# Cross-attention block on one core: the last tile of context keys in three passes instead of five, and a new hand-written order of the loop and its ends

## The reference, cut to what matters

```python
def _attn(x, ctx, wq, wk, wv, wo, bo, heads):
    q, k, v = x @ wq, ctx @ wk, ctx @ wv        # split into heads
    sim = jnp.einsum('bhid,bhjd->bhij', q, k) * scale
    a = jax.nn.softmax(sim, axis=-1)
    out = jnp.einsum('bhij,bhjd->bhid', a, v)
    return out @ wo + bo                        # heads joined again
h1 = _ln(x, n1_g, n1_b)
x = _attn(h1, h1, q1, k1, v1, o1_w, o1_b, heads) + x
h2 = _ln(x, n2_g, n2_b)
x = _attn(h2, context, q2, k2, v2, o2_w, o2_b, heads) + x
h3 = _ln(x, n3_g, n3_b)
a, g = jnp.split(h3 @ ff_w1 + ff_b1, 2, axis=-1)
return a * jax.nn.gelu(g, approximate=False) @ ff_w2 + ff_b2 + x
```

## Time and profile before

| | us |
|---|---|
| three runs: median, lowest, highest | 1290.41, 1287.4, 1293.53 |
| the profiled execution: its own time | 1285.88 |
| its span, first to last instruction | 1284.1 |
| PE busy in it | 1224.0 |
| first self scores of the lead-in, of the loop, first exponent of the run-out, first matmul of the feed-forward stage (from the span's start) | 147.93, 191.36, 860.03, 924.05 |

### The profile page before, as it was taken

The page is one execution under the profiler, slowest core; times in us unless marked ns, Lnnn a source line. Parts: engine busy times, 40 slices in busy tenths (PEclk is TensorE's granted clock), DMA queues, the critical chain, the costliest instruction groups (busy, mean ns, idle before and its releaser), DMA issues. The chain is left out here.

```text
span 1284.1 us, 34279 instructions
## 1 busy us (share of the span) xinstructions
PE 1224.0 (95%) x12788; PEld 1127.6 (88%) x12788; DVE 814.2 (63%) x1606; ACT 668.2 (52%) x1622; POOL 601.2 (47%) x792
## 2 busy tenths in 40 slices
PE   5899879999999999999999999998899999999999
PEld 3898768989898888888888988886699999999999
DVE  5554457888787788887888888876565243332521
ACT  5565326666666666666666666664552322323130
POOL 5431235465564654655646556451673433423331
PEclk9999879999999999999999999999899999999999
DMA  4576744544545555455454554532121101010000
GB/s 129 194 237 210 240 155 122 166 152 143 170 139 178 163 156 183 151 167 181 129 174 134 153 165 130 178 107 78 41 63 36 31 11 41 0 51 0 26 1 26
DMA packets 105145, 154.49 MB, mean 120 GB/s; under 512 B 20780, under 2 KB 86564, under 8 KB 104996
## 3 DMA queue, kind: packets, MB, share of 16 engines
q1 hardware_dynamic: 104556, 151.94, 38.2%
q10 hardware_dynamic: 440, 0.54, 0.1%
HBM read 62.98 MB, written 28.93 MB: 72 GB/s over the span
## 5 line engine op out<-in xcount | busy, mean ns | idle before, releaser
L1418 ACT ACTIVATE probs<-expin 120x400 f32<-120x400 f32 (+2 forms) x635 | 293.3, 505 | 132.3 <-PE expin L811 130.3
L1095 DVE TENSOR_REDUCE neg_max<-score 100x2 f32<-100x722 f32 x320 | 288.2, 901 | 100.6 <-PE score L785 99.2
L811 PE MATMUL expin<-qs,ks 128*120 128x200 f32 (+2 forms) x1270 | 197.0, 272 | 6.3 <-ACT probs L1418 3.0
L811 PEld LDWEIGHTS expin<-qs,ks 128*120 128x120 f32 (+2 forms) x1270 | 176.4, 180 | 16.8 <-ACT probs L1418 5.8
L785 PE MATMUL score<-ks,qs 128*100 128x362 f32 x640 | 172.6, 351 | 11.8 <-DVE neg_max L1095 7.4
L1609 POOL MEMSET qs<- 128x2400 f32 (+1 forms) x58 | 112.6, 1941 | 146.5 <-PE expin L811 146.5
L2664 DVE SCALAR_TENSOR_TENSOR hidden<-ps_a,b_cols,gelu 128x320 f32<-128x320 f32 x100 | 55.1, 551 | 166.1 <-PE ps_a L2588 166.0
L2826 POOL TENSOR_TENSOR hid_lo<-hidden,hid_hi 128x320 fp32r<-128x320 f32 x100 | 88.1, 881 | 122.0 <-ACT hid_hi L2734 121.8
L2746 ACT ACTIVATE gelu<-ps_g,b_cols 128x320 f32<-128x320 f32 x100 | 52.7, 527 | 137.8 <-PE ps_g L2588 137.8
L785 PEld LDWEIGHTS score<-ks,qs 128*100 128x100 f32 x640 | 83.6, 166 | 38.4 <-issue 21.0
L833 PE MATMUL attn<-probs,vc 120*17 120x100 f32 (+1 forms) x3840 | 107.9, 251 | 0.0
(11 more groups left out here) (222 smaller groups left out, 2893.1 us busy)
## 6 DMA issues: line engine op xcount, KB each, us to landing
ks<-kc_parts SPq DMA_DIRECT2D x96, 362.0 KB, 4.0
qk_dram<-qk_parts SPq DMA_DIRECT2D x32, 500.0 KB, 5.5
qs<-q_parts SPq DMA_DIRECT2D x192, 75.0 KB
ks<-qk_dram SPq DMA_DIRECT2D x96, 125.0 KB
ctx_raw<-in_ctxT SPq DMA_DIRECT2D x64, 180.5 KB
ks<-kc_parts SPq DMA_DIRECT2D x96, 90.5 KB, 2.7
qs<-qk_dram SPq DMA_DIRECT2D x64, 125.0 KB
vs<-v_dram SPq DMA_DIRECT2D x32, 132.8 KB
```

The lines of the kernel that those rows point to most:

```text
L811: mm = pe.matmul(dst, ks[a][u][:, k_slot(c) if a == 2 else c, j0:j0 + n], qs[a][u][:, :, q_slot(c) if a == 2 else c, :], start=True, stop= ...
L1095: ins = nc.vector.tensor_reduce(dst, src, AX_X, ALU.max, negate=True)
L1418: nc.scalar.activation(probs[e % NPT][0:n, :], expin[e % 2][0:n, 0:HG * N], ACT.Exp, scale=SCALE)\
```

## The change: what it does, and its diff

The weights of the context lie in a new layout: four pieces (high and low of the first 128 features, high twice and low twice of the last 64) for key tiles 0 and 1 and for the values, and a piece of its own, `w_c_last`, for key tile 2. The context's second column block holds its high part in partitions 0 to 63 and its low part in 64 to 127 ("mixed"), and `ctx_lo` has the first 128 features alone. Key tiles 0 and 1 and the values still take five passes. Key tile 2 takes three: high and low weights side by side (128 columns held) against the high context, the high weights (64 columns) against the low context, and 128 columns against the mixed block. Its sum then lies in two halves of the PSUM bank, and DVE adds them with one more instruction in `kc_low`. POOL makes the mixed block with one more instruction for each part of a context.

All five engines get another order. In the loop, self-attention's exponents of groups 0 to 3 of f stand at the end of f's period, not at the start of the next one, and so does the turn of s's maxima; `project_vc(s, 2)` and `turn_max(1, f)` stand between the second self scores and the first cross scores. The lead-in and the run-out are reordered too.

```diff
 def work_jobs(x, s, c, f):
-    order = [("MT2", x, 0), ("VC", s, 2), ("O2", y, 0), ("MT1", f, 0), ("KC", c, 0), ("KC", c, 1), ("O1", c, 0),
-             ("KC", c, 2), ("T2", c, 0), ("Q2", c, 0), ("QT", c, 0), ("VC", c, 0), ("VC", c, 1)]
+    order = [("VC", s, 2), ("MT1", f, 0), ("O2", y, 0), ("KC", c, 0), ("O1", c, 0), ("KC", c, 1), ("T2", c, 0),
+             ("KC", c, 2), ("Q2", c, 0), ("QT", c, 0), ("VC", c, 0), ("VC", c, 1), ("MT2", s, 0)]
...
+        w_c = [at("w_c", [P, 8 * P + 4 * D], early.weights), sb("w_c_last", [P, 2 * P], F32R)]
...
             def run_out():                                        # SP
+                place_kc(30, 0)
                 place_kc(30, 2)
                 place_q2(30)
...
             def period(x, s, c, f, e):                            # SP
                 y = x - 1 if x else None
+                v = y - 1 if y else None
+                place_kc(s, 0)
                 place_q2(s)
                 place_max(2, x)
-                if x is not None and 8 <= x < 8 + FF // P:
-                    load_w1(x - 8)
+                if y is not None and 8 <= y < 8 + FF // P:
+                    load_w1(y - 8)
+                place_kc(s, 2)
+                place_max(1, f)
                 load_context(f)
-                place_kc(s, 2)
+                store_x2(v)
                 load_qkv1(e)
-                load_x(e)
-                place_kc(c, 0)
-                store_x2(y)
-                place_max(1, f)
+                load_x(f)
...
             def project_kc(b, t):                                 # PE
-                dst = bank(job)[0:f1 - f0, 0:JP]
-                pe.matmul(dst, w_c[:, 0, f0:f1], ctx_hi[:, 0, :], start=True, stop=False)
-                pe.matmul(dst, w_c[:, 1, f0:f1], ctx_hi[:, 0, :], start=False, stop=False)
-                pe.matmul(dst, w_c[:, 0, f0:f1], ctx_lo[:, 0, :], start=False, stop=False)
-                pe.matmul(dst, w_c[:, 2, f0:f1], ctx_hi[:, 1, :], start=False, stop=False)
-                done(pe.matmul(dst, w_c[:, 2, f0:f1], ctx_lo[:, 1, :], start=False, stop=True), job)
+                m, hi, lo, mixed = f1 - f0, ctx_hi[:, 0, :], ctx_lo[:], ctx_hi[:, 1, :]
+                dst = bank(job)[:, 0:JP]
+                if t == 2:
+                    w = w_c[1]
+                    pe.matmul(dst[0:2 * m], w[:, 0:2 * m], hi, start=True, stop=False)
+                    pe.matmul(dst[0:m], w[:, 0:m], lo, start=False, stop=False)
+                    mm = pe.matmul(dst[0:2 * m], w[:, 2 * m:4 * m], mixed, start=False, stop=True)
+                else:
+                    passes = ((0, hi), (1, hi), (0, lo), (2, mixed), (3, mixed))
...
             def lead_in():                                        # PE: its start
+                project_out(1, 0)
                 self_scores(1, 0)
-                project_out(1, 0)
+                self_scores(1, 1)
                 project_kc(0, 0)
                 project_vc(0, 0)
                 project_kc(0, 1)
-                self_scores(1, 1)
+                turn_normalised(0)
                 turn_max(1, 1)
-                turn_normalised(0)
                 project_q2(0)
                 turn_q2(0)
+                project_vc(0, 1)
                 self_scores(2, 0)
...
             def run_out():                                        # PE: its start
-                scores_for_exp(1, 31, 0, 0)
-                turn_max(2, 29)
-                scores_for_exp(1, 31, 1, 0)
-                scores_for_exp(1, 31, 2, 0)
-                scores_for_exp(1, 31, 3, 0)
                 scores_for_exp(1, 31, 4, 0)
...
                 project_vc(30, 2)
+                project_out(2, 28)
                 cross_scores(30, 0)
-                project_out(2, 28)
...
             def period(x, s, c, f):                               # PE
                 self_scores(f, 0)
-                scores_for_exp(1, c, 0, 0)
-                turn_max(2, x)
-                scores_for_exp(1, c, 1, 0)
-                project_vc(s, 2)
-                scores_for_exp(1, c, 2, 0)
-                scores_for_exp(1, c, 3, 0)
-                self_scores(f, 1)
                 scores_for_exp(1, c, 4, 0)
                 times_v(1, c, 0)
...
                 times_v(1, c, 4)
+                self_scores(f, 1)
+                project_vc(s, 2)
+                turn_max(1, f)
                 cross_scores(s, 0)
                 project_out(2, y)
-                turn_max(1, f)
-                cross_scores(s, 1)
                 scores_for_exp(2, x, 0, 0)
                 scores_for_exp(2, x, 0, 1)
+                cross_scores(s, 1)
                 project_kc(c, 0)
                 scores_for_exp(2, x, 0, 2)
                 scores_for_exp(2, x, 1, 0)
                 cross_scores(s, 2)
+                project_out(1, c)
+                scores_for_exp(2, x, 1, 1)
+                cross_scores(s, 3)
+                scores_for_exp(2, x, 1, 2)
                 project_kc(c, 1)
-                scores_for_exp(2, x, 1, 1)
-                scores_for_exp(2, x, 1, 2)
-                cross_scores(s, 3)
-                project_out(1, c)
                 scores_for_exp(2, x, 2, 0)
                 scores_for_exp(2, x, 2, 1)
                 cross_scores(s, 4)
+                times_v(2, x, 0)
+                times_v(2, x, 1)
+                scores_for_exp(2, x, 2, 2)
+                cross_scores(s, 5)
+                scores_for_exp(2, x, 3, 0)
+                turn_normalised(c)
+                scores_for_exp(2, x, 3, 1)
                 project_kc(c, 2)
-                scores_for_exp(2, x, 2, 2)
-                scores_for_exp(2, x, 3, 0)
-                times_v(2, x, 0)
-                cross_scores(s, 5)
-                scores_for_exp(2, x, 3, 1)
+                cross_scores(s, 6)
                 scores_for_exp(2, x, 3, 2)
-                turn_normalised(c)
-                times_v(2, x, 1)
-                cross_scores(s, 6)
                 scores_for_exp(2, x, 4, 0)
                 project_q2(c)
                 cross_scores(s, 7)
...
                 times_v(2, x, 4)
+                scores_for_exp(1, f, 0, 0)
                 cross_scores(s, 9)
+                scores_for_exp(1, f, 1, 0)
                 project_vc(c, 0)
+                scores_for_exp(1, f, 2, 0)
                 project_vc(c, 1)
+                scores_for_exp(1, f, 3, 0)
+                turn_max(2, s)
...
             def kc_low(b, t):                                     # DVE
...
+                hi, lo = kc_parts[0:m, 0, t, :], kc_parts[0:m, 1, t, :]
+                n = link(nc.vector.tensor_tensor(lo.bitcast(F32), src[0:m], hi.bitcast(F32), ALU.subtract))
+                dve.wait_ge(dve_step, n)
+                nc.vector.tensor_tensor(lo, src[m:2 * m], lo.bitcast(F32), ALU.add)\
+                    .then_inc(work_empty[WORK_AT[job][0]], 1)
...
             def period(x, s, c, f):                               # DVE
+                max_low(2, x)
                 maximum(1, f, 0)
-                max_low(2, x)
                 turn_back(2, y)
                 maximum(1, f, 1)
+                turn_heads(1, c)
                 maximum(2, s, 0)
-                turn_heads(1, c)
+                turn_back(1, c)
                 maximum(2, s, 1)
+                max_low(1, f)
                 result(y)
-                turn_back(1, c)
                 maximum(2, s, 2)
-                max_low(1, f)
                 kc_low(c, 0)
-                kc_low(c, 1)
+                second_input(c)
                 maximum(2, s, 3)
-                second_input(c)
                 statistics(c)
                 maximum(2, s, 4)
                 normalise(c)
                 maximum(2, s, 5)
+                kc_low(c, 1)
                 features_low("T2", c)
                 maximum(2, s, 6)
                 kc_low(c, 2)
...
             def split_part(j):                                    # POOL
-                hi, lo, raw = ctx_hi[:, :, j], ctx_lo[:, :, j], ctx_raw[:, :, j]
+                hi, lo, raw = ctx_hi[:, :, j], ctx_lo[:, j], ctx_raw[:, :, j]
                 link(nc.gpsimd.tensor_tensor(hi, raw, one[:].unsqueeze(2).broadcast_to(list(raw.shape)), ALU.mult))
-                return nc.gpsimd.tensor_tensor(lo, raw, hi.bitcast(F32), ALU.subtract)
+                mixed = hi[64:P, 1]
+                link(nc.gpsimd.tensor_tensor(mixed, raw[64:P, 1], mixed.bitcast(F32), ALU.subtract))
+                return nc.gpsimd.tensor_tensor(lo, raw[:, 0], hi[:, 0].bitcast(F32), ALU.subtract)
...
                 y = x - 1 if x else None                          # POOL, loop body
-                first_residual(f)
-                scale_products(2, y)
-                split_first(c)
                 heads_low(2, y)
                 split_last(c)
                 scale_products(1, c)
...
                 clear_cross(c)
+                first_residual(f)
                 second_residual(c)
+                scale_products(2, x)
```

(52 more changed lines are left out.)

254 lines of the change are left out of this document (131 added, 123 removed), and 13 rows, old and new, of the table DRAIN_EXP.

## The result

The changed kernel takes 1306.6 us (median of 4 runs, 1303.5 to 1307.93) beside 1291.53 for the kernel before on the same chip: a ratio of 1.0131, 95% interval 1.0102 to 1.0159. It is 1.3% slower. The forecast was 1280 us and faster, with 1297 as the upper end of its range. The two profiled executions lie further apart than the medians, 22.05 us (1307.93 and 1285.88): that of the kernel before was 5.6 us under its median, so the differences between the two profiles overstate the loss by some 7 us.

A forecast was written before the change was run, and what follows sets the result against it. PE was taken to bound the loop, except one 2.04 us step set by DVE's maximum. Loop -5, lead-in -2 and run-out -3 gave -10 us: 1290.41 - 10 = 1280 us, range 1266 to 1297.

The forecast's parts named there:

- A step that never varies is set by the maximum: Loop, second self scores to first cross scores: 2.04 us, set by DVE's maximum whatever PE does meanwhile.
- The passes: Key tile 2 loses two passes of 0.165 us for each of 32 sequences, 10.6 us in all.
- is gone: Key tile 2 in the loop: two passes fewer take 0.33 us off each period.
- so I take nothing: POOL's third split instruction: 1.23 to 2.45 us for two halves, costed at nothing as the first part starts a period earlier.
- I cost it at nothing: DVE's second step of `kc_low`, before cross score 8: 0.6 us a period uncovered, taken as covered by PE's other work.
- The wait behind self score 1: PE, second self scores to first cross scores: 1.34 us of work in 2.04, so it waits 0.70.
- forecast floor: First to second self scores cannot take under 2.04 us; PE's work there is 1.91, a wait of 0.13.
- The irregular part: Mean period less quiet period, 0.28 us, linked to waits on SP's placements; expected to change by -0.15 (0 to -0.28).
- the loop's sum: Loop: -0.02 us a quiet period and -0.15 irregular, 29 x -0.17 = -5 us.
- the loop's lower end: Most favourable bound for the loop, given as 29 x (-0.46) = -13 us.
- The slower rival: Score chain: POOL's longer split delays scaling, so PE waits 0.6 us a period for DVE's maxima; 1297 us, chance 0.15.
- The ends: Lead-in -2 us (0 to -4) and run-out -3 us (-1 to -6), from moved work and reordering.

The follow-up runs named there:

- e1: Kernel before with the new weights' layout, three passes and the split in three instructions, old order kept: 1296.92 us, ratio 1.0035.
- e5: e1 with POOL's split in two instructions by a mask (the masked split), old order: 1291.14 us, ratio 0.9976.
- e12: e9 without DVE's second instruction of `kc_low` for key tile 2, leaving out part of its low sum: 1282.29 us, ratio 0.9933.
- e2: Kernel before with only the new order on every engine, five passes and the old two-instruction split: 1304.1 us, ratio 1.0088.
- e7: Changed kernel with POOL's split in two instructions by a mask: 1299.6 us, ratio 1.0047.
- e10: e7 with POOL's `clear_own(e)` behind `heads_low(1, c)` and SP's `load_x(f)` ahead of `load_context(f)`: 1284.65 us, ratio 0.9951.
- e11: Kernel before with only SP's `place_max(1, f)` moved ahead of `place_kc(c, 0)` and `store_x2(y)`: 1284.8 us, ratio 0.9948.
- e9: e5 with SP's `place_max(1, f)` moved ahead of `place_kc(c, 0)` and `store_x2(y)`: 1282.02 us, ratio 0.9927.

## Why the prediction was wrong

- **What bounds the kernel.** "A step that never varies is set by the maximum" was right for that step, and I took PE for the pace of all others since no wait showed there. A wait of nothing is not slack: `project_kc(c, 0)` followed the end of the split by 0.22 us. e1 took 0.32 us from PE and the period did not change.
- **The passes** have the length that was forecast: 0.51 us for three, 0.17 each; the 131 ns that the Trainium skill, "TensorE: Matmul & The Clock Gate", section "Back-to-back issue gap", gives for 512 columns are not reached here at 362. That 0.33 us a period "is gone" held only where the two added instructions were out of the way: nothing arrives with the split in three (e1), 0.21 in two (e5), 0.30 without DVE's second step as well (e12 against before), and some 0.3 in the new order (e2 to e7, less POOL's 0.10). In time it was 2.8 and some 5 us, not 10.6.
- **The step that failed: POOL's third instruction, "so I take nothing".** Its size was inside the bounds: 0.70 + 0.71 us for 480 elements (1.23 as one instruction) and 0.44 + 0.45 for 244. Its cover was wrong. I named `split_first` as moved to the end of the period before, and did not follow what stands behind it in POOL's list: `heads_low(2, ·)`, for which DVE's `turn_heads(1, c)` waits. Beside the masked split it costs about 0.6 us a period in the changed order (e7, 0.84% of the time) and 0.2 in the old one (e5). That is nearly the whole miss in the quiet period: forecast 22.76, measured 23.44, and 22.87 without it. The Trainium skill, "GPSIMD Engine Reference", section "2.1 Instruction dispatch", says that each core of that engine works on its own 16 partitions; the rows agree, since 64 partitions by 240 took 0.70 and 128 by 240 took 0.71, so a half-height instruction saves nothing.
- **DVE's second step, "I cost it at nothing".** It costs 0.10 us in the old order (e12), against a bound of 0.6 without cover. In the changed order no wait shows there.
- **The wait behind self score 1** was right: 0.72 against 0.70. From self score 0 to 1 the forecast floor was 2.04; it is 1.94, so that 0.13 did not come. Not foreseen: a turn of maxima takes 0.12 and 0.18 us at its two new places, against 0.03 at both old ones.
- **The irregular part** was forecast to shrink by 0.15 and did, by 0.10 (23.61 less 23.44, before 23.07 less 22.80). That was luck: the long quiet period hid SP's late `load_x(f)`, which the forecast did not name, and with a shorter one the part is 0.46 (e7). With the third instruction gone, `clear_own` later and x early (e10) the quiet period is 22.71 and the mean 22.83, against 22.76 and 22.89 in the forecast; so the loop's sum came out once these were out of the way, and what e10 still lacks to 1280 us lies in the ends (last period and run-out 91.4 us, before 86.7).
- **A slip in the sum.** By the bounds of its own terms the loop's lower end is 29 x (-0.52) = -15 us, not 29 x (-0.46); nothing else hangs on it.
- **The slower rival** had the right list: `turn_heads(1, c)` ahead of maximum 0, all on one PSUM tile. I hung it on the scaling and on maximum 1, and argued against it with DVE's free fifth. The lateness came from POOL, and a second wait with it, 0.40 us at O(1,c), whose heads stand behind `clear_own`. The Trainium skill, "Perfetto Trace Analysis", section "Identifying the Most-Contended Engine", says to optimize the engine with the highest occupancy first, and for TensorE to judge by the weight loads' share (587 of 684 us here, still the highest); here the work that lengthened the period stood on an engine that is busy 55%, and the measurement decides.
- **The ends.** Forecast -2 and -3. The lead-in gained nothing (+0.1). The run-out lost 5.8 us in this profile. Over all profiles, the last period and run-out take 90.9 to 93.1 us in the seven kernels with the changed order and three passes, and 87.4 to 90.4 in the four with the old order and three passes. The kernel before takes 86.7, but with only SP's order changed (e11) 88.6, and the new order with five passes (e2) 89.5, so which part of the change makes the run-out longer is not shown. In the changed kernel PE is busy 57.55 us there for 633 matmuls, 50.78 for 643 before. A row of its timeline and three stretches of the windows (the granted clock is the third column from the end):

```profile
901.64 0.73 PE L803 MATMUL score<-ks,qs 128*100 128x362 f32 x2 [1.76 <-DMA qs<-q_parts]
```

```profile
900.00:905.00 5.00, 3.35 (x13) 3.19 (x14) 3.62 (x7) 0.73 (x3) 0.75 (x1) 0.68 0.19 59
910.00:915.00 5.00, 4.76 (x37) 3.59 (x36) 2.79 (x4) 2.86 (x6) 0.82 (x1) 0.50 0.71 110
930.00:935.00 5.00, 4.81 (x58) 3.58 (x58) 1.01 (x3) 2.65 (x6) 4.92 (x6) 0.50 0.00 0
```

PE waits 1.76 us for the queries of sequence 31, and the mean clock from 900 to 905 is 0.68; it waits twice 1.00 us for a maximum (905 to 909), and the clock from 910 to 915 is 0.50, the 1.2 GHz level, and again from 930 to 935. The kernel before, with the clock at 1.00 until 920, had its own idle places there, so which of the moved steps brings the clock down was not tried and stays open.

## What to carry to other kernels

Before costing an added instruction at nothing, follow its engine's list to the next instruction for which another engine waits, and compare the two arrival times: a consumer that started 0.22 us after its producer had next to no slack here, whatever the busy shares said. Take work from an engine only after finding the ring that sets the period; moving one instruction of known length into a suspected stretch shows whether the ring goes through it. On an in-order DMA queue, put first what is waited for first: one moved line on SP was worth 6.7 us here (e11), more than the passes.

## What was not expected of the hardware

- A POOL tensor_tensor has a fixed part: 240 elements took 0.70 us and 122 took 0.45, so 2.1 ns an element and about 0.19 us besides. Two halves cost 0.2 us more than the whole.
- A transpose of one small tile on PE takes 0.03 us from start to start behind an output projection or between products for exponents, 0.12 where PE had waited for it (550.62 to 550.74), and 0.18 ahead of self scores (546.46 to 546.64).
- Shorter quiet periods did not shorten the others as much: in e5 PE waits 9.9 us in the loop for the rows of the maxima, 1.6 with SP's order changed (e9). How much longer the long periods became is not shown, since e5's profile is of its slowest execution.
